# A routed-expert phase on one core: the gather and scatter engine paced by another product, two scatters a step, and the rows to scatter loaded by the other queue

## The reference

```python
x = x + xattn(layernorm(x), ctx, ctx, mask, Wq, Wk, Wv, Wo, 16)
# ffn, on xt = layernorm(x) as rows of 256 features
scores = sigmoid(xt @ gate_w.T)
_, idx = lax.top_k(scores + gate_b, 4)
w = take_along_axis(scores, idx, axis=-1)
w = w / sum(w) * 2.5
for e in range(16):                      # w13[e]: 256 x 256, w2[e]: 256 x 128
    y += comb[:, e] * (silu_and_mul(xt @ w13[e].T) @ w2[e].T)
y = y + silu_and_mul(xt @ w13_s.T) @ w2_s.T
x = x + y
```

## Time and profile before

| | |
|---|---|
| median of three runs | 2229.42 us (2228.61 to 2232.89) |
| the profiled execution | 2215.58 us, its span 2213.7 us |
| mean granted clock of PE | 0.988 of full speed |
| expert phase | from about 1570 us of the span to its end |
| busy over the span | PE 2085.0, DVE 1866.6, ACT 1674.1, POOL 1413.7 us |

### The profile page before, as it was taken

One profiled execution on the slowest core, in us unless ns is written; L12 is line 12 of the kernel. 1 busy time (PEld: TensorE's weight loads), 2 busy tenths in 40 slices (PEclk: granted clock), 3 DMA queues, 4 the chain that ended last, 5 costly groups with the idle time before them and its releaser, 6 DMA issues. The chain is left out here.

```text
span 2213.7 us, 57965 instructions
## 1 busy us (share of the span) xinstructions
PE 2085.0 (94%) x16512; PEld 2006.2 (91%) x16512; DVE 1866.6 (84%) x6129; ACT 1674.1 (76%) x4795; POOL 1413.7 (64%) x2107
## 2 busy tenths in 40 slices
PE   7999999999999999999999999999899898898885
PEld 6999999999999998999999998999789888888884
DVE  7999999999999999999999999999854446676777
ACT  6989889888888988898888888888655544544532
POOL 4565655555555555888788877876555556666655
PEclk9999999999999999999999999999999999999998
DMA  7777777777777766866666665666667668887897
GB/s 208 185 182 191 186 176 188 184 180 192 178 188 182 184 167 170 223 181 179 177 175 173 184 169 156 174 175 173 225 245 258 246 243 277 288 282 272 278 315 254
DMA packets 261295, 457.32 MB, mean 207 GB/s; under 512 B 36544, under 2 KB 148672, under 8 KB 260992
## 3 DMA queue, kind: packets, MB, share of 16 engines
q1 hardware_dynamic: 235376, 383.07, 61.8%
q0 software_dynamic: 25616, 70.55, 10.0%
HBM read 141.00 MB, written 144.70 MB: 129 GB/s over the span
## 5 line engine op out<-in xcount | busy, mean ns | idle before, releaser
L792 POOL TENSOR_SCALAR E<-E,rinv 128x256 f32<-128x256 f32 x1024 | 482.3, 482 | 468.4 <-DVE rinv L1105 463.8
L980 ACT ACTIVATE E<-E,negmax 128x256 f32<-128x256 f32 x1024 | 508.7, 502 | 6.4 <-DVE negmax L1130 6.3
L1130 DVE CUSTOM_DVE_ANT_0 E<-pS,m_in 128x256 f32<-128x256 f32 x1024 | 387.2, 415 | 33.1 <-PE pS L889 30.1
L1149 DVE TENSOR_TENSOR PT_lo<-pT,PT_hi 128x512 fp32r<-128x512 f32 x512 | 350.6, 685 | 28.2 <-ACT PT_hi L998 23.5
L1598 POOL DMA_INDIRECT block<-expert_rows,slot x256 | 248.6, 971 | 149.5 <-issue 58.9
L998 ACT ACTIVATE PT_hi<-pT 128x512 fp32r<-128x512 f32 x512 | 304.8, 595 | 9.4 <-PE pT L899 0.6
L899 PE MATMUL pT<-ident,E 128*128 128x128 f32 x2048 | 307.1, 272 | 0.6 <-POOL E L792 0.6
L912 PE MATMUL pV<-PT_hi,V 128*128 128x256 f32 x1024 | 287.5, 303 | 6.5 <-DVE PT_lo L1149 6.5
L964 ACT ACTIVATE qk_sp<-pj 128x256 fp32r<-128x256 f32 x512 | 197.0, 385 | 108.8 <-PE pj L87 93.2
L888 PE MATMUL pS<-qk_st 128*128 128x256 f32 x1024 | 269.0, 284 | 8.1 <-DMA qk_st<-qk_sp 7.7
L889 PE MATMUL pS<-qk_st,qk_sp 128*128 128x256 f32 x1024 | 266.5, 282 | 0.0
(11 more groups left out here) (266 smaller groups left out, 6890.7 us busy)
## 6 DMA issues: line engine op xcount, KB each, us to landing
qk_st<-qk_sp SPq DMA_DIRECT2D x512, 192.0 KB
qk_st<-qk_sp SPq DMA_DIRECT2D x512, 128.0 KB
sorted_rows<-qk_st SPq DMA_DIRECT2D x152, 256.0 KB, 3.5
xg<-sorted_rows SPq DMA_DIRECT2D x76, 512.0 KB
expert_rows<-block SPq DMA_DIRECT2D x76, 512.0 KB
acc<-x_plus_attention SPq DMA_DIRECT2D x35, 256.0 KB
x_in<-in_x SPq DMA_DIRECT2D x32, 256.0 KB
c_in<-in_ctxT SPq DMA_DIRECT2D x32, 256.0 KB, 4.0
```

The costliest lines, as they stand in the source:

```text
L792: last = pool.tensor_scalar(e[:, t, :], e[:, t, :], rinv[:, r, t:t + 1], 1.0, ALU.mult, ALU.mult)
L980: last = act.activation(E[r][:, t, :], E[r][:, t, :], ACT.Exp, bias=negmax[:, r, t:t + 1], scale=-1.0, accum_out=rowsum[:, r, t:t + 1])
L1130: last = dve.tensor_tensor_reduce(out=E[r][:, t, :], in0=pS[g % 2][:, t, :], in1=m_in.tile(b)[:, t, :], scale=-1.0, scalar=BIG, op0=ALU.ad ...
L1149: dve.tensor_tensor(lo[:, :, :], pT[n % 2][:, :, :], f32(hi[:, :, :]), ALU.subtract).then_inc(s_ptlo, 1)
```

## The change

- `keep_pace(i)` waits for s_y in place of s_GU, and for `worked(i - 4)`: POOL's step i starts when PE has finished `down` of unit i - 5, which stands in PE's step i - 1.
- A batch is scattered in 4 steps in place of 4.5, two scatters in each of steps 11 to 66 (before: one or two in steps 11 to 73).
- `load_to_scatter` moves from POOL to SP, three steps ahead of the batch's first scatter (steps 8, 12, 16, ... 56), behind the load of sorted rows and the store of expert rows of that SP step. Its waits go with it.

```diff
-    BATCH_STEPS = 4.5
-    scatter_at = {}
+    BATCH_STEPS = 4
+    scatter_at, fetch_at = {}, {}
...
             at = max(at, PLACE_AT + 8 + 3 * (b - GROUP_START[g]))
+        if b != LAST:
+            fetch_at.setdefault(int(at) - 3, []).append(b)
...
         @block.sync
...
+            def load_to_scatter(b):
+                n = b - scattered
+                if n >= 2:
+                    shared.scattered_here(sp, b - 2)
+                else:
+                    sp.wait_ge(s_w13lo, N_EXP)
+                sp.wait_ge(shared.s_xnout[b % 2], DMA * (b // 2 + 1))
+                sp.dma_start(to_scatter[n % 2], rows_of(shared.xn_rows[b])).then_inc(s_toscat[n % 2], DMA)
...
                     store_sorted(i - 5)
+                for b in fetch_at.get(i, ()):
+                    load_to_scatter(b)
                 for use in stores_at.get(i, ()):
...
         @block.gpsimd
...
-            def load_to_scatter(b):
...
             def keep_pace(i):

-                if worked(i - 1):
-                    pool.wait_ge(s_GU, worked(i - 1))
+                if worked(i - 4):
+                    pool.wait_ge(s_y, worked(i - 4))
...
-                if i == SCATTER_FROM - 1:
-                    for b in range(scattered, scattered + 2):
-                        load_to_scatter(b)
...
-                    if t + j == 0 and scattered < b < LAST - 1:
-                        load_to_scatter(b + 1)
```

## The result

The changed kernel takes 2210.89 us (median of four runs, 2207.7 to 2211.4) where the kernel before takes 2229.02 us on the same chip: ratio 0.9913, 95% interval 0.9896 to 0.9931. That is 0.87% **faster**, 18 us. The forecast was 2236.0 us and slower, its range 2225 to 2243: wrong, in sign and in range.

A forecast was written before the change was run, and what follows sets the result against it. PE (busy 94%) was taken to set the time, and at the end the chain from last gathers over last combine to its store. Terms 1.0 + 0 + 5.6 = 6.6 us on 2229.42 gave 2236.0 us, range 2225.0 to 2243.0.

The forecast's parts named there:

- The loads that leave POOL: Scatters: taking 13 loads and their 36.0 us of idle time off POOL gains 0, as POOL idles at releases anyway.
- Two scatters a step: Scatters 12% denser, ending in step 66 instead of 73: price 0, as POOL needs 2.5 us of each 3.20.
- First load: SP's step 8: the first moved load waits for the last weight split, delaying DVE's addition; +1.0 us, bounds 0 and 2.2.
- Later release in the middle: Gather steps released one period, 6.2 to 7.55 us, later: price 0, covered by COMBINE's four steps; upper bound 3 us.
- rival (b): Gathers not there in time, so DVE waits: 10 to 16 us more, about 2246 to 2252; chance 0.06.
- Later release at the end: Last six gathers wait for the last `down`, taken as 2204.7, and start 5.6 us later, all on the path: +5.6 us.
- The alternative +4.6: End: with a gather landing 2.3 us from its start, the last combine starts 1.0 us sooner, +4.6 in place of +5.6.
- Rival (c): Gathers issued later within the pair leave the way to SP's transfers: faster, 2219 if all 17 us come back; chance 0.12.
- Carrying the difference: The profiled execution was 13.8 us under the median, so the +6.6 us was added to the median 2229.42.

The follow-up runs named there:

- late_load: Kernel before, with POOL loading the next block ahead of a block's fourth scatter instead of its first: 0.9943, 0.9937 and 0.9938 of before on three chips.
- no_pace: Changed kernel with the old release (wait for s_GU of the step just back) put back: 2212.63 us, 0.9969 of before.
- dense_only: Kernel before with only 4 steps a block instead of 4.5, two scatters in each step: 2230.13 us, 1.0048 of before.
- loads_only: Kernel before with only the loads of rows to scatter moved to SP's queue: 2198.15 us, 0.9905 of before; on another chip 0.9942.
- loads_pace: Changed kernel with 4.5 steps a block as before, so without the denser scatters: 0.9953 and 0.9946 of before on two chips.
- pace_only: Kernel before with only the later release, POOL waiting for s_y of the step four back: 2215.82 us, 0.9977 of before.
- early_gather4: Changed kernel with gathers scheduled 4 steps behind their group's last sorted step instead of 7: 0.9980 of before.
- before_again: Kernel before, unchanged, run once more for its profile on another chip: 2136.16 us in one execution.

## Why the prediction was wrong, step by step

- **"The loads that leave POOL ... worth 0": the step that failed.** The argument was that "POOL is idle at releases anyway" and that "nobody waits for POOL". It was read from the gathers and carried over to the scatters. The rows for it were there: 36.0 us idle ahead of 13 loads, of which 5.2 are DVE's, so 2.8 us ahead of each of the 11 others. Added up for one batch, 9.9 + 2.8 + 0.9 is 13.6 us against 14.4, hardly any spare time. In its place the runs show: on the chips at 2137 to 2139 POOL is 1.6 us a batch too slow, the first gather stands behind that on POOL's queue, and the row of gathers behind it keeps its length (9 to 15 us; late_load alone does it). On chip A the same loads are worth 22 us, by another way: POOL keeps up with PE up to the last scatter there, and what changes is PE's sorted step, 3.11 us in no_pace against 3.43 in dense_only, which differ in the loads alone (and 2.96 in loads_only against 3.20 in before, from the chip at 2229). Why PE is slower stays open.
- **"Two scatters a step ... price 0, covered by POOL's idle time"** was wrong on chip A: dense_only costs 10 us, and no_pace is 14 us above loads_only. The missing cover is not what the trace of dense_only shows, since POOL stands idle for 19.75 us ahead of its first gather; again PE's step is longer (3.43 us). With the loads gone and the later release it costs nothing on chips B and D (loads_pace against the changed kernel: +0.1 and +2.3 us, inside the intervals).
- **First load +1.0:** a wait of 1.49 us for the accumulator. Right in mechanism and size, and irrelevant.
- **Later release in the middle, 0:** no DVE wait for gathers in the middle (the sign of rival (b) appears at the end only, the 7.2 us above); the gathers' row is 2.2 us longer, inside the bound of 3. On its own the release gave 4 us on chip A, a gain that the text had left possible and not priced.
- **Later release at the end, +5.6:** measured 0; in the trace of the changed kernel PE is done at 2190.8, before POOL gets there. The term took PE's end as given, and the release seems to move it. The four traces with the old release on the chips at 2220 and 2229 all have a long drain of PE (8.4, 9.7, 5.6 and 5.6 us) and a last addition 3.8 to 5.6 us behind the one before; the two with the later release have 2.0 and 1.9 us, and 2.6. On the chips at 2137 to 2139 the drain is 1.0 to 2.0 us with either. So the late last product at 2204.7 is no chance of one execution, but it goes with the old release; how is not shown. Of loads_only and pace_only:

```profile
L1316 PEldq DRAIN  x1: 9745/9745/9745, 2177.0 to 2177.0; - x1
```

```profile
L1314 PEldq DRAIN  x1: 1912/1912/1912, 2193.7 to 2193.7; - x1
```

- **The alternative +4.6** has a slip: by its own numbers the combine could start at 2205.0 + 6.29 + 2.3 = 2213.6, which is 1.2 us sooner and makes +4.4.
- **Rival (c), faster, 0.12:** right in sign only. Its sign, 1780 matmuls in 250 us of gathers, is absent (1736); the gain lies in the scatters, of which it said nothing.
- **Carrying the difference:** the profiled execution of before was 13.4 us under the median, and I took that as constant. The 18 us are measured between medians, and the pair of traces shows 4.

## What to carry to other kernels

Add up the work of the queue that issues transfers for one period of the pipeline, its waits for its own transfers included, and hold it against the period. An engine that waits for its own last transfer looks idle in the profile and is not; moving that wait three issues further back was worth the whole change here on the faster chips. And look for the first instruction behind which everything keeps its length, here the first gather, and for what it waits: on one kind of chip it was POOL's own row, on the other PE's pace. It is a guide and no law: early_gather4 started the first gather a little earlier, and the row behind it grew.

## What the hardware showed that was not expected

- The same kernel took 2229, 2220 and 2137 to 2139 us on different chips, with nearly equal granted clocks (0.988 and 0.992), and the traces are alike in the first 1400 us (10844 and 10831 matmuls, a DMA share of 0.71 in both): the difference lies in the expert phase. Each chip was used once, so it can't be told from the time of the run. The 256 gathers take 394 us on the one kind and 329 on the other, with the DMA engines at 0.82 and 280 GB/s and at 0.97 and over 338 GB/s (the stretch 1812 to 2080 us of before_again, next row). A gain of one version over another is worth little without before on the same chip.

```profile
1812.00:2080.00 268.00, 263.33 (x2217) 259.50 (x2216) 220.60 (x495) 155.51 (x361) 202.75 (x208) 1.00 0.97 338
```

- A scatter's landing is no fixed number: where the profile doesn't name PE as what the load behind it waited for, the load starts 1.97 to 4.06 us after the last scatter's row ended in the trace of before, and 3.1 to 4.7 us after it in before_again. From the row's start it is 2.9 us in the earlier trace rows and 4.5 us in the first lines of before_again. The Trainium skill (DMA: Bandwidth & Descriptors, Anatomy of one DMA) has by the prediction's estimate 2.3 us from the start for 128 KB; neither trace agrees. For the last gather the estimate is nearer: the combine that waits for it starts 2.80 us behind its row's start (2202.26 and 2205.06 above).
